# A two-layer graph network on one Trainium2 core: both node products of the first layer in one matmul of 128 columns per block

## What is computed

```python
all_feat = concatenate([x[dst], x[src], edge_attr, u_per_node[dst]], axis=-1)
msg = relu(all_feat @ W1 + b1)
agg = segment_sum(msg, dst, num_segments=n)
node_in = concatenate([x, agg, u_per_node], axis=-1)
x1 = layernorm(x + relu(node_in @ W2 + b2))
```

## Time and profile before

| | |
|---|---|
| median of 3 runs | 15650.02 us (15645.94 to 15651.08) |
| the profiled execution, by the same clock | 15667.31 us |
| its span in the trace | 15665.6 us |
| busy share PE / PEld / DVE / ACT / POOL | 44% / 37% / 32% / 3% / 60% |
| first edge loop starts (DVE clears `by_rank`) | 390.54 us |
| node stage of the first pass, first transposes to last normalization | 5945.1 to 6128.5 us |

### The profile page before, as it was taken

One profiled execution on the slowest core, in us unless ns is written; L12 is line 12 of the kernel. 1 busy time (PEld: TensorE's weight loads), 2 busy tenths in 40 slices (PEclk: granted clock), 3 DMA queues, 4 the chain that ended last, 5 costly groups with the idle time before them and its releaser, 6 DMA issues.

```text
span 15665.6 us, 128029 instructions
## 1 busy us (share of the span) xinstructions
PE 6858.2 (44%) x29865; PEld 5870.1 (37%) x29865; DVE 4970.4 (32%) x12980; ACT 396.2 (3%) x790; POOL 9376.9 (60%) x9927
## 2 busy tenths in 40 slices
PE   3555665666666565333333333334333333333333
PEld 3455555555555555222222222223222222222222
DVE  1333333333333333233233323233332233233223
ACT  0000000000000000000000000000000000000000
POOL 5555555555555554666666666665666666666664
PEclk9666666556565655555555555555555555555555
DMA  2233333333333332111111212112111111111111
GB/s 57 65 67 67 68 68 67 67 68 68 67 69 67 67 69 47 34 34 34 34 34 34 34 34 35 34 34 46 24 23 23 23 23 23 23 23 23 23 23 33
DMA packets 1678916, 688.51 MB, mean 44 GB/s; under 512 B 1375841, under 2 KB 1518977, under 8 KB 1678734
## 3 DMA queue, kind: packets, MB, share of 16 engines
q1 hardware_dynamic: 1363181, 359.16, 11.0%
q0 software_dynamic: 315680, 328.70, 10.9%
HBM read 658.74 MB, written 28.14 MB: 44 GB/s over the span
## 4 chain that ended last, share of the span: by engine, by line
another core or an unknown queue 47%; DVE 18%; DVEq 14%; issue 11%; PE 8%; POOL 1%; DMA 0%; SPq 0%; ACT 0%; ACTq 0%; POOLq 0%
DVE by_rank L940 13%; DVEq L909 11%; PE sum_ps L653 4%; DVE hit L925 3%; PE pre_ps L630 1%; PE pre_ps L627 1%; DVEq L933 1%; DVEq L930 1%; DVEq L925 1%; DVEq L931 1%; POOL ranked L528 1%; DVE summed_in L919 1%; DVE scratch L913 0%; DVEq L335 0%
## 5 line engine op out<-in xcount | busy, mean ns | idle before, releaser
L546 POOL DMA_INDIRECT rows<-source_table,index x6250 | 5927.0, 948 | 4120.7 <-issue 2000.2
L940 DVE TENSOR_TENSOR by_rank<-by_rank,sum_ps 64x128 f32 (+1 forms) x9375 | 2626.0, 280 | 7858.2 <-remote 6978.5
L653 PE MATMUL sum_ps<-hit,message 128*64 128x128 f32 (+1 forms) x12500 | 2844.0, 404 | 3493.7 <-DVE hit L925 1462.8
L546 POOL DMA_INDIRECT message<-source_table,index x3125 | 2955.6, 946 | 1639.9 <-issue 888.1
L653 PEld LDWEIGHTS sum_ps<-hit,message 128*64 128x64 f32 (+1 forms) x12500 | 2375.0, 237 | 3845.3 <-issue 3780.9
L653 PE MATMUL sum_ps<-hit,rows 128*64 128x128 f32 x6250 | 1428.3, 412 | 3091.1 <-DVE hit L925 2056.6
L653 PEld LDWEIGHTS sum_ps<-hit,rows 128*64 128x64 f32 x6250 | 1205.0, 218 | 3314.1 <-issue 3307.4
L925 DVE TENSOR_TENSOR hit<-out_ps,edge_place 128x640 f32<-128x640 f32 x1875 | 1539.6, 821 | 1349.2 <-issue 1201.9
L627 PE MATMUL pre_ps<-w_edge,scratch 96*128 96x192 f32 x2500 | 983.0, 487 | 1356.3 <-DVE summed_in L919 867.9
L630 PE MATMUL pre_ps<-scratch 128*128 128x64 f32 x6250 | 1331.5, 360 | 462.0 <-issue 461.8
L630 PEld LDWEIGHTS pre_ps<-scratch 128*128 128x128 f32 x6250 | 1298.6, 280 | 538.9 <-issue 511.5
(11 more groups left out here) (156 smaller groups left out, 1413.5 us busy)
## 6 DMA issues: line engine op xcount, KB each, us to landing
rows<-source_table,index POOLq DMA_INDIRECT x6250
scratch<-ranked SPq DMA_DIRECT2D x3125, 32.0 KB
scratch<-place_rows SPq DMA_DIRECT2D x625, 160.0 KB
scratch<-in_edge_t_steps SPq DMA_DIRECT2D x625, 96.0 KB
message<-in_edge_steps SPq DMA_DIRECT2D x625, 80.0 KB
message<-source_table,index POOLq DMA_INDIRECT x3125
xt<-in_x_t SPq DMA_DIRECT2D x28, 224.0 KB
index<-in_src_steps SPq DMA_DIRECT2D x375, 12.5 KB
```

Source lines behind the costliest of these rows:

```text
L546: nc.gpsimd.indirect_dma_start(to, None, source_table[l][:, :], bass.IndirectOffsetOnAxis(ap=index[:, at.j, s:s + 1], axis=0))\
L653: one = mm(tile_sum(at.half, s)[0:w, :], (message if l < 2 else rows)[:, at.slot, s, 0:w], hit[:, at.half, s, :], start=True, stop=True)
L940: V.tensor_tensor(at_rank[s], at_rank[s], tile_sum(at.half, s)[0:w, :], ALU.add)\
```

## The change

The source half and the destination half of a block come from one matmul with all 128 columns of `w_ab`. The global row goes in as row 65 of the weights: `xt` gets a 65th partition of ones, and `w_ab` and `w_2x` a 65th row. That row is worked out once: PE multiplies `glob_b` by both `w_glob` into `out_ps`, and DVE copies partition 64 of it to row 64 of `w_ab` (the source half of that row is zero) and of `w_2x`. The node stage of the first pass uses the same 65 rows, so its third product per block goes as well. Numbers of products: 294 before and 98 after in the node-product stage, 294 before and 196 after in the node stage, and two new ones at the start.

```diff
-        w_ab = sb("w_ab", [F, 2 * F])
+        w_ab = sb("w_ab", [F + 1, 2 * F])
-        w_2x = sb("w_2x", [F, F])
+        w_2x = sb("w_2x", [F + 1, F])
-        xt = sb("xt", [F, 2, GB * P])
+        xt = sb("xt", [F + 1, 2, GB * P])
...
-                sp.dma_start(xt[:, h, :], a["x_t"][:, g * GB * P:(g + 1) * GB * P]).then_inc(xt_in[h], 16)
+                sp.dma_start(xt[0:F, h, :], a["x_t"][:, g * GB * P:(g + 1) * GB * P]).then_inc(xt_in[h], 16)
...
             pe.wait_ge(globals_ready, 1)
+            mm(out_ps[:, 0:F], glob_b[:, :], w_glob[0][:, :], start=True, stop=True)
+            mm(out_ps[:, F:2 * F], glob_b[:, :], w_glob[1][:, :], start=True, stop=True).then_inc(globals_ps, 1)
+            pe.wait_ge(globals_kept, 1)
             for g in range(NG):
...
                 for q in range(GB):
-                    xb = xt[:, h, q * P:(q + 1) * P]
-                    mm(to[:, q * P:q * P + F], xb, w_ab[:, 0:F], start=True, stop=False)
-                    mm(to[:, q * P:q * P + F], glob_b[:, :], w_glob[0][:, :], start=False, stop=True)
-                    last_mm = mm(to[:, q * P + F:(q + 1) * P], xb, w_ab[:, F:2 * F], start=True, stop=True)
+                    last_mm = mm(to[:, q * P:(q + 1) * P], xt[:, h, q * P:(q + 1) * P], w_ab[:, :], start=True, stop=True)
...
-                                mm(to, xt[:, h, q * P:(q + 1) * P], w_2x[:, :], start=False, stop=False)
-                                one = mm(to, glob_b[:, :], w_glob[1][:, :], start=False, stop=True)
+                                one = mm(to, xt[:, h, q * P:(q + 1) * P], w_2x[:, :], start=False, stop=True)
...
             V.tensor_copy(glob_b[0:G, :], glob[:, 0:1].to_broadcast([G, P])).then_inc(globals_ready, 1)
+            V.memset(xt[F:F + 1, :, :], 1.0)
+            V.memset(w_ab[F:F + 1, F:2 * F], 0.0)
+            dve.wait_ge(globals_ps, 1)
+            V.tensor_copy(w_ab[F:F + 1, 0:F], out_ps[F:F + 1, 0:F])
+            V.tensor_copy(w_2x[F:F + 1, :], out_ps[F:F + 1, F:2 * F]).then_inc(globals_kept, 1)
```

More of the change, by code:

```diff
@@ L199, in build @@
         globals_ready = sem("globals_ready")
+        globals_ps = sem("globals_ps")
+        globals_kept = sem("globals_kept")
         ab_done = sem("ab_done")
@@ L365, in _ @@
             loads = [
-                (w_ab[:, 0:F], a["L0_gnn_W1"][0:F, :]), (w_ab[:, F:2 * F], a["L0_gnn_W1"][F:2 * F, :]),
+                (w_ab[0:F, 0:F], a["L0_gnn_W1"][0:F, :]), (w_ab[0:F, F:2 * F], a["L0_gnn_W1"][F:2 * F, :]),
                 *((w_edge[n * C:(n + 1) * C, n * F:(n + 1) * F], a["L0_gnn_W1"][2 * F:2 * F + C, :]) for n in range(STACK)),
@@ L369, in _ @@
                 (w_glob[0][G:G + 1, :], a["L0_gnn_b1"].unsqueeze(0)),
-                (w_2x[:, :], a["L0_gnn_W2"][0:F, :]), (w_2a[:, :], a["L0_gnn_W2"][F:2 * F, :]),
+                (w_2x[0:F, :], a["L0_gnn_W2"][0:F, :]), (w_2a[:, :], a["L0_gnn_W2"][F:2 * F, :]),
                 (w_glob[1][0:G, :], a["L0_gnn_W2"][2 * F:2 * F + G, :]),
@@ L472, in _ @@
                                 sp.wait_ge(node_out[0], g - 1)
-                            sp.dma_start(xt[:, g % 2, :], a["x_t"][:, g * GB * P:(g + 1) * GB * P])\
+                            sp.dma_start(xt[0:F, g % 2, :], a["x_t"][:, g * GB * P:(g + 1) * GB * P])\
                                 .then_inc(xt2_in[g % 2], 16)
```

## The result

The changed kernel takes 15529.62 us (median of 4 runs, 15517.63 to 15557.87), the kernel before 15647.98 us (4 runs, 15625.24 to 15651.08). The ratio is 0.9934, with a 95% interval of 0.9921 to 0.9947: 118 us less, 83 to 124 by the interval. The forecast was 15569, 81 us less. The profiled execution took 15557.87 us against 15667.31 before, 109.4 us less. The four runs of the kernel before are the three of the table and one more, and that one is the 15625.24; against it alone the changed kernel is 96 us faster.

The account below looks back on a forecast made before the run. PE's products were taken to bound the path in the node-product stage, held beside POOL's gathers, and in the first pass's node stage. Terms -66 and -15 gave -81, from the median 15650 to 15569 us, range 15525 to 15638.

Parts of the forecast that it names:

- The pass: Node-product stage: one pass of 128 columns by 128 weights takes 0.213 us, at most 0.427 if weights and columns add up.
- The groups, -66: Node-product stage: 14 shorter groups end near 190.5 us and not at 256.7, 66 us gained; bounds -50 and -91.
- the stretch: Held stretch in the node-product stage, about 70 to 171 us: PE passes slow and signals held beside POOL's unbroken gathers.
- ACT doesn't see group 8 until 171: Node-product stage: PE's signal for group 8 is held until 171 us, so SP cannot load `xt` for group 10.
- PE runs group 9 slowly: Node-product stage: inside the held stretch PE does group 9 at a slow rate, one pass each 2.6 us.
- The node stage, -15: First pass's node stage: 14 of 42 passes per group removed, 15 us gained; bounds 0 and -42.
- the slower rival: Node stage: gathers never pause, PE's passes fall into a held stretch, the stage grows by 131 us; 15700 us, chance 0.04.
- The halved 29 us: Node stage: 2.5 us per group in some 12 groups makes 29 us; half was taken because POOL would have no break.
- Edge loops, 0 with 10 either way: Edge loops and later passes: same instructions and buffers, so 0, with 10 us either way for another phase at the start.
- No held stretch in the first stage: Rival: the shorter node-product stage escapes the hold and ends before `first` at 164.9; 15544 down to 15517 us, chance 0.13.
- Recording alone: Rival: profiling makes the held stretch, so unprofiled runs gain only in the node stage; 15635 down to 15608 us, chance 0.10.
- A property of the program as it runs: Held signals beside unbroken gathers, seen also in the first edge loop, were taken as general and not of one place.

Follow-up runs that it names:

- e5: The changed kernel again, unedited, on a second chip where the kernel before takes 15650.88 us: 15568.3 us, ratio 0.9948.
- e7: The changed kernel with the node stage back at three products per block, so only the node-product stage changed: 15552.03 us, ratio 0.9955 to the kernel before.
- e12: The changed kernel with earlier `xt` loads; in every second first-edge-loop step POOL waits until the previous step's gathers have landed: 13306.56 us, ratio 1.0473.
- e9: The kernel before, with POOL's gathers of destination rows broken by a pause of some 4 us after each seven: 15560.06 us (one run).
- e8: The changed kernel with the node-product stage back at three products per block, so only the node stage changed: 15598.84 us, ratio 0.9986.
- e1: Only the node-product stage changed, on a chip where the kernel before takes 12677.57 us: 12680.04 us, ratio 1.0001.
- e4: The changed kernel, with POOL waiting for all 14 groups of node products before the first gather of destination rows: 12727.96 us (one run).
- e10: The changed kernel, with POOL in all three edge loops waiting until the previous step's gathers have landed: 16366.23 us, ratio 1.0478.

## Why the prediction was right, and where it wasn't

**The start cost nothing**, as said: PE's first group waits for `xt` until 36.10 (35.64 before).

**The pass was 0.223 us**, taken at 0.213. The row decides against the upper bound of 0.427. The Trainium skill, page "TensorE: Matmul & The Clock Gate", section "The mechanism", lets a weight load, in its list of what overlaps, overlap only a matmul of another row group, which would have made the group 6 us; all passes of L596 use the same 65 rows, a group takes 3.12, and the measurement decides.

**The groups, -66.** The stage ended at 188.2 (190.5 said), `place` came at 193.7 (196), the clearing at 321.5 (324): -69.0, and -65 to -66 in e5 and e7. The mechanism held in its main line: the stretch is set by the gathers, it meets the stage near group 8, and what is left at 171 runs behind it. What happens inside the stretch was wrong. "ACT doesn't see group 8 until 171" failed: signals came, each 30 to 65 us late (copies at 98, 137, 172), so SP could load group 9 at 99.41 and group 10 at 138.82, and PE did them at 103.12 and 142.99. "PE runs group 9 slowly" failed as said, for all groups in the stretch ran at 3.36 us; but the rate behind it, one pass each 2.6 us, is about that at which whole groups are passed on. With one group less behind 171, the end came 2 us sooner than said. The run of gathers was also read too short. It begins at 25.27 and not at 52.97:

```profile
25.27 1.10 POOL L520 DMA_INDIRECT xn<-in_dst_rows,tile_of  x1 [21.35 <-DVE tile_of L836]
...
46.18 4.45 POOL L520 DMA_INDIRECT xn<-in_dst_rows,tile_of  x1 [0.30 <-issue]
```

From there on POOL is idle for 0.3 us between gathers, though four of them (35.43 to 50.93) last 1.7 to 6.5 us. So "13 gathers into that run", on which e12 also builds, is no count after which a hold begins.

**The node stage, -15.** It was -13.7, and -9 where nothing is held. The size was right and the reasoning was not. "PE's period becomes 8.9 us, under POOL's 9.5" failed: two products per block run at 0.304 us per pass, so the 28 take 8.5 us and not 6.0. From the second transposes to the last it is 149.4 us before and 135.2 after, 14.2 less. The period fell by 0.7 us (12.0 to 11.3), 8 us of this, and the other 6 are the two held groups, each 3 us longer before. They are gone beside a POOL that keeps its breaks; in e7, with three products, one of them is there. "But then POOL has no break" never came up, so the slower rival wasn't tried. The halved 29 us hit by two errors that cancelled.

**Edge loops, 0 with 10 either way.** Too narrow. First to last gather of the first loop is 5498 us before and 5456 to 5487 in the changed kernel and e5 to e9, with the same instructions; the profiled pair differs by 20.6 us there. Between the two comparisons of the same kernels, -118 and -83, the start can't be the difference, since it repeats within 3 us. Of the 35 us, 22 go with the choice of runs of the kernel before: against its fourth run the first comparison is -96. The rest no trace places, since the profiled executions of the changed kernel differ by 8.5 us alone. The total of 0 stands by e5 and by e7 and e8, whose gains (68 and 21) are those of the stages (65, and 8 to 11) and a few more.

**The rivals.** No held stretch in the first stage: fell by ACT's rows, there; in e1 to e4 it is the rule. Recording alone: fell by e7, whose four runs without a profile are 63 to 80 us under the kernel before, from a stage that would otherwise be worth nothing. The Trainium skill, page "NOTIFIC — the notification-queue block", section "Interfaces", offered a way for records to stall an engine; no run here shows it at work.

**"A property of the program as it runs"** was the largest error, without effect on this number. The same program takes 12678 us in one group of runs and 15648 in another, and where it takes 12678 the change is worth 0.0 to 0.1%, by its parts (the whole was not run there). Each group was on its own chip, once, so whether it is the chip or the occasion isn't shown, and what makes the difference stays open. The forecast holds only where PE is held beside the gathers as in the profile before.

## What to carry to other kernels

Before work is cut from an engine, ask what it waits for there: 196 products less were worth 66 us only because they let the stage get through eight of its 14 groups before, and three more within, a stretch in which all that PE passes on is late, and nothing where there is no such stretch. Long runs of indirect DMAs without a break are suspect when another engine's signals come late; a break every few gathers shows whether they are the cause, and what the break costs has to be paid in any case. A saving per instruction must be measured in its new order: fewer passes can each become longer.

## What was not expected of the hardware

- The kernel before took 15620 to 15651 us on some chips and 12678 to 12705 on others (each chip once), 23% more at the granted clock of 1.00 in the node-product stage of both. The first edge loop is 5498 us in one and 3925 in the other.
- Beside 73 instructions of POOL in 101 us PE did 39 passes on the one, and its signals came up to 105 us apart; beside 72 in 91 us it did 428 on the other. The signals of ACT and SP's loads were not late. The rate is 1.40 us per instruction of PE, weight loads counted. A break of 4.2 us or more in each seven gathers ended it (e9), and so did one of about 2 us in each five (e10).
- A product with 64 rows and one with 65 in turn run at 0.304 us per pass (L690, L691), products with 65 rows only at 0.223 us (L596), products with 64, 64 and 33 rows in turn at 0.218 us (42 passes in 9.16 us). The Trainium skill, page "TensorE: Matmul & The Clock Gate", section "LDWEIGHTS (loading the stationary operand)", has the load depend on the columns alone and not on the rows. The 33 rows among the 64 agree; the change from 64 to 65 and back doesn't. But the granted clock differs too: it is 0.50 (1.2 GHz) in the node stage of either kernel and 1.00 (2.4 GHz) in the stage of L596. The windows of the node stage (columns as in the earlier trace rows), before and after:

```profile
5974.00:6001.00 27.00, 21.84 (x100) 20.70 (x99) 9.40 (x18) 2.41 (x4) 13.75 (x17) 0.50 0.20 51
5874.00:5990.00 116.00, 104.30 (x361) 83.97 (x360) 49.75 (x96) 14.24 (x22) 68.99 (x80) 0.50 0.24 61
```

  The products with 64, 64 and 33 rows take 0.21 to 0.22 us at either clock, so the clock alone doesn't explain 0.304; products with 65 rows only were not run at 0.50. No run isolates it; a 65th row of `cat_t` would.
